# Second routed layer: the output projection made token-major in three passes, its additions on DVE

## The chip, the cores and the metric

The kernel runs on one core of a Trainium2 chip. The metric is the time of one execution in device microseconds (us), the median of several runs. The engines are PE (matrix products), DVE (vector), ACT (activations), POOL (general purpose) and SP, which issues the transfers.

## The reference, cut to what matters

The program is eight sublayers that add to x, 16 batch elements of 256 tokens of 128 numbers, 4096 tokens in all. The sixth one, the second routed layer, is concerned here. Each token has a routing weight rw for each of 16 experts, and every expert has 128 x 128 matrices for Q, K, V and the output:

```python
q = jnp.einsum('btc,ech,bte->bth', hidden_states, q_proj, rw)
k = jnp.einsum('btc,ech,bte->bth', hidden_states, k_proj, rw)
v = jnp.einsum('btc,ech,bte->bth', hidden_states, v_proj, rw)
scores = jnp.einsum('bqh,bkh->bqk', q, k) * scale      # causal, then a softmax over k
ao = jnp.einsum('bqk,bkh->bqh', attn, v)
out = jnp.einsum('bth,ehc,bte->btc', ao, o_proj, rw)   # added to x
```

## The kernel before

`layer2_ffn` works on groups of four tiles of 128 tokens, 512 tokens; there are eight groups (`ITERS`), j = 0 to 7. Each engine runs its own list of instructions in order, and they meet by counting signals. `run_mains` writes `main` out for the first two and the last two groups and loops over the four between.

In `main(j)` a loop over the experts e = 0 to 15 makes Q, K and V. PE spreads the routes of expert e over all partitions (`spread`, L1799, into one of the two banks psR), two experts ahead. DVE multiplies the transposed tokens by them (`scale_by`, L1980, into a ring of four buffers xs). ACT rounds the product to a high part xsh (L1727), and DVE writes the low part, xs - xsh (`low_part`, L1984), one expert later than the scaling. PE then adds nine products of 512 columns, three for each of Q, K and V: low weights by high tokens, high by low, high by high (L1865). Expert 0 has no parts: it takes three float32 products (L1860). Between the experts DVE makes the routes of the next group, in pieces at e = 6, 7, 8, 9, 11 and 13 (`front_gate` and what follows), and PE transposes for the next group at e = 2, 4 and 14.

After the loop comes the output projection of the group before, `mix_o(j)`. Again PE spreads the routes (a copy that POOL keeps, L1681), DVE scales the transposed attention result aoT by them, and PE makes one float32 product of 512 columns for each expert into psX (L1843). Put between these experts (`stages`) are the steps of this group's attention: scores, transposed V, the maxima and the normalised probabilities on DVE, their transposes, the product with V; and then, on DVE, the normalisation of group j + 2 (`front_ln`, `front_xn`, `front_norm`). ACT stores psX as oT, PE transposes it back to token-major at e = 10 of a later group (`out_T`, L1793), and DVE adds it to x (`add`, L2005). A last `mix_o(8)` stands behind the last group.

The weights are loaded during the attention sublayer that comes before (`narrow_attention`): SP starts the loads after its first `stack` of queries, and POOL makes the high and low parts of the Q, K and V weights (`Ahead.split`, L134 and L136) after its own last group.

Of the kernel before, what the change touches and what calls it, by code (L numbers as in the profile page):

```python
# [5 lines left out]
F32 = mybir.dt.float32  # L6
# [60 lines left out]
class Program:  # L67
# [19 lines left out]
    "dve_steps", "pool_steps", "act_steps", "ahead", "split", "up_scaled", "up_ready", "ctx_high", "ctx_split", "n_split", "q_split", "k_split", "khat_first", "x_split", "x_high", "x_loaded", "weights_qk", "inputs", "out_stored",  # L87
# [22 lines left out]
class Ahead:  # L110


    def __init__(self, tensors, loads, copies=(), splits=()):
        self.tensors, self.loads, self.copies, self.splits = tensors, loads, tuple(copies), tuple(splits)

    def __add__(self, other):
        return Ahead({**self.tensors, **other.tensors}, self.loads + other.loads, self.copies + other.copies,
                     self.splits + other.splits)
# [3 lines left out]


# [5 lines left out]
    def split(self, pr, pool):  # L129

        if self.splits:
            pool.wait_ge(pr.sig("ahead").sem, pr.sig("ahead").at(16 * len(self.loads)))
        for k, (raw, hi, lo) in enumerate(self.splits):
            pr.nc.gpsimd.tensor_copy(hi, raw).then_inc(pr.sig("split").sem, 1)  # L134
            pool.wait_ge(pr.sig("split").sem, pr.sig("split").at(k + 1))
            pr.nc.gpsimd.tensor_tensor(lo, raw, hi, ALU.subtract)  # L136

    @property
    def counts(self):
        return dict(ahead=16 * len(self.loads), split=len(self.splits))  # L140
# [447 lines left out]
def narrow_attention(pr, x_sb, common, dram, layer, wt, ahead):  # L588
# [7 lines left out]
    with ExitStack() as ctx:  # L596
# [28 lines left out]
        def _(sp):  # L625
# [18 lines left out]
            for j in range(ITERS):  # L644
                stack(j)
                if not j:
                    ahead.start(pr, sp)
                if masked and j + 1 < ITERS:
                    load_mask(j + 1)

        @block.gpsimd
        def _(pool):
# [14 lines left out]
            ahead.split(pr, pool)  # L667
# [903 lines left out]
def layer2_ffn_weights(nc, ctx, dram):  # L1571
    sb = buffers(nc, ctx, "f2w")
    E = L2_E
    t = {k: sb(k, [P, E, P]) for k in ("wq", "wk", "wv", "wo")}
    t.update(sim=sb("sim", [P, E]), ones=sb("ones", [P, P]), sg=sb("sg", [P, E]), desc=sb("desc", [P, E]),
             tri32=sb("tri32", [P, P]), tri=sb("tri", [P, P], BF16), self32=sb("self32", [P, E * P]),
             selb=sb("selb", [P, E * P], BF16))
    for k in ("wq", "wk", "wv"):
# [3 lines left out]
                     (t["tri32"][:], dram["tri"]), (t["self32"][:], dram["F2_sel"])] +  # L1582
                    [(t[k][:], dram["F2_" + k]) for k in ("wq", "wk", "wv", "wo")],
                 [(t["selb"][:], t["self32"][:]), (t["tri"][:], t["tri32"][:])],
                 [(t[k][:], t[k + "h"][:], t[k + "l"][:]) for k in ("wq", "wk", "wv")])


def layer2_ffn(pr, x_sb, common, wt):
# [8 lines left out]
    with ExitStack() as ctx:  # L1597
        def sb(name, shape, dt=F32):
# [3 lines left out]
        wq, wk, wv, wo, sim, ones, sg, tri, desc, selb = (wt[k] for k in ("wq", "wk", "wv", "wo", "sim", "ones", "sg", "tri",  # L1602
                                                                         "desc", "selb"))
# [9 lines left out]
        rwTo = sb("rwTo", [P, T4], BF16)  # L1613
# [7 lines left out]
        aoT, oT = sb("aoT", [P, 2, T4]), sb("oT", [P, T4])  # L1621
# [4 lines left out]
        psX = ctx.enter_context(nc.psum_tensor("psX_f2", [P, T4], F32))  # L1626
        psY = ctx.enter_context(nc.psum_tensor("psY_f2", [P, T4], F32))
        psA = psQKV + [psY]
# [7 lines left out]
        def qn(j, e):  # L1636
            return e if isinstance(j, int) and j == 0 else 2 * E * j - E + e

        def on(j, e):
            return 2 * E * j + e - (E if isinstance(j, int) and j == ITERS else 0)  # L1640


        def split_no(j, e):
            return (E - 1) * j + e - 1
# [21 lines left out]
        def _(pool):  # L1666
# [10 lines left out]
            def keep_routes(j, q):  # L1677

                pool.wait_ge(s("gate_bcast").sem, s("gate_bcast").at(2 * E * j + E))
                pool.wait_ge(s("gate_parts").sem, s("gate_parts").at(j + 1))  # L1680
                nc.gpsimd.tensor_tensor(rwTo[:].rearrange("e (c t) -> e c t", t=P), rwTb[:, q, :].rearrange("e (c t) -> e c t", t=P),  # L1681
                                        ones[:].unsqueeze(1).broadcast_to([P, TPI, P]), ALU.mult)\
                    .then_inc(s("routes_kept").sem, 1)

            def main(j, q):
                if has_second_next(j):
                    front(j + 2)
                keep_routes(j, q)
# [5 lines left out]
        def _(act):  # L1694
# [17 lines left out]
            def front_parts(j, q):  # L1712
                act.wait_ge(s("gate_T").sem, s("gate_T").at(j + 1))
                if not is_first(j, 2):
                    act.wait_ge(s("routes_kept").sem, s("routes_kept").at(j - 1))
                nc.scalar.activation(rwTb[:, q, :], psM[:], ACT.Copy).then_inc(s("gate_parts").sem, 1)

            def store_o(j):

                act.wait_ge(s("hidden").sem, s("hidden").at(on(j, E)))  # L1720
                act.wait_ge(s("ffn_outT_ready").sem, s("ffn_outT_ready").at(j - 1))
                nc.scalar.activation(oT[:], psX[:], ACT.Copy).then_inc(s("ffn_outT").sem, 1)

            def main(j, q):
                for e in range(1, E):
# [13 lines left out]
                for c in range(TPI):  # L1739
                    nk = P * (c % 2 + 1)  # L1740
                    act.wait_ge(s("maxed").sem, s("maxed").at(j * TPI + c + 1))
                    nc.scalar.activation(p[:, c, 0:nk], psA[c][:, 0:nk], ACT.Exp, bias=nmax[:, c:c + 1],
# [3 lines left out]
                for c in range(TPI):  # L1746
                    nk = P * (c % 2 + 1)
# [832 lines left out]
```

## Time and profile before

| | us |
|---|---|
| median of 3 runs | 2017.27 (2017.11 to 2026.06) |
| the profiled execution, its own time | 2015.44 |
| its span | 2013.3 |
| PE busy in the span | 1626.2 (81%) |
| DVE busy | 1284.4 (64%) |
| ACT busy | 926.6 (46%) |
| POOL busy | 210.0 (10%) |
| second routed layer, first instruction to last addition | about 1058 to 1613 |

Busy is the time in which an engine has an instruction under way. A matmul's record ends some time after the next one may start, so starts are compared rather than durations added. A float32 product of 512 columns is two records; a product of the rounded parts is one. The granted clock is the share of PE's full clock, 2.4 GHz; 0.50 is 1.2 GHz.

### The profile page before, as it was taken

To read this page: it belongs to the slowest core of one execution; us is meant where nothing else is said; L and a number is where in the kernel's file an instruction comes from. 1 tells how busy PE (TensorE), PEld (TensorE's weight loads), DVE (VectorE), ACT (ScalarE), POOL (GpSimd) and SP (SyncE) were. 2 spreads that over 40 slices of the span, in tenths; PEclk is the share of its full clock that TensorE was granted. 3 is DMA by queue.
4 is the path that set the end of the run, shared out by engine and by line. 5 is a ranking of instruction groups with operands and counts; after the bars stand their busy time and mean duration, and the time that the engine had idled before them with its cause. 6 is when DMAs were issued, how large, how long until landed. Compare 5 with 4: busy or idle time off the path is not lost. (4 is left out here: it accounts for less than half of the span.)

```text
span 2013.3 us, 27147 instructions
## 1 busy us (share of the span) xinstructions
PE 1626.2 (81%) x8633; PEld 1104.1 (55%) x8633; DVE 1284.4 (64%) x2870; ACT 926.6 (46%) x1759; POOL 210.0 (10%) x188
## 2 busy tenths in 40 slices
PE   6999938978869999978975899999999968848004
PEld 5777726855546666645653656656666445523004
DVE  4777771147657667646765566666665548776985
ACT  3555523356635565545551322222222146626862
POOL 2110020011200000011131000000000011010320
PEclk9999967959979999979996999999999969969557
DMA  4000000032100000023210000000000012100000
GB/s 149 1 1 0 0 1 0 0 112 47 39 1 0 1 0 0 1 91 104 60 26 0 1 1 0 1 1 0 0 1 0 0 50 50 43 0 0 0 0 42
DMA packets 23456, 41.71 MB, mean 21 GB/s; under 512 B 7720, under 2 KB 11184, under 8 KB 22320
## 3 DMA queue, kind: packets, MB, share of 16 engines
q1 hardware_dynamic: 23344, 40.32, 6.8%
q8 instruction: 58, 0.95, 0.2%
q14 instruction: 54, 0.44, 0.1%
HBM read 19.32 MB, written 2.10 MB: 11 GB/s over the span
## 5 line engine op out<-in xcount | busy, mean ns | idle before, releaser
L962 DVE TENSOR_REDUCE mP_a<-psY_a 128x8 f32<-128x512 f32 x192 | 128.2, 688 | 118.8 <-PE psY_a L800 117.9
L720 ACT ACTIVATE probs_a<-psX_a 128x512 f32<-128x512 f32 x192 | 109.1, 595 | 149.0 <-PE psX_a L827 148.3
L1727 ACT ACTIVATE xsh_f<-xs_f 128x512 fp32r<-128x512 f32 x120 | 75.8, 632 | 202.8 <-DVE xs_f L1980 202.6
L1980 DVE TENSOR_TENSOR xs_f<-xT_f,psR_f 128x512 f32<-128x512 f32 x128 | 86.9, 686 | 83.1 <-PE psR_f L1799 75.3
L1843 PE MATMUL psX_f<-xs_f,wo_f2w 128*128 128x512 f32 x256 | 128.6, 594 | 0.0
L2375 PE MATMUL ps_f<-wT_f,xq_f 128*128 128x128 f32 x192 | 24.5, 292 | 125.4 <-DVE xq_f L2396 125.4
L1980 DVE TENSOR_TENSOR xs_f<-aoT_f,psR_f 128x512 f32<-128x512 f32 x128 | 85.8, 685 | 61.6 <-PE psR_f L1799 61.4
L1507 DVE SCALAR_TENSOR_TENSOR g_f<-psU_f,cols_f1w,t_f 128x512 f32<-128x512 f32 (+1 forms) x104 | 77.9, 749 | 73.2 <-ACT t_f L1320 71.0
L800 PE MATMUL psY_a<-ks_a,xs_a 96*128 96x256 f32 x384 | 100.7, 367 | 28.0 <-DMA xs_a<-ql_a 16.3
L1402 PE MATMUL psO_f<-h_f,w_f1w 128*128 128x512 f32 (+1 forms) x208 | 107.6, 599 | 0.0
L1320 ACT ACTIVATE t_f<-psU_f,cols_f1w 128x512 f32<-128x512 f32 (+1 forms) x104 | 71.2, 684 | 76.0 <-PE psU_f L1386 76.0
L800 PEld LDWEIGHTS psY_a<-ks_a,xs_a 96*128 96x128 f32 x384 | 69.0, 215 | 59.6 <-issue 20.9
L827 PE MATMUL psX_a<-xs_a,ks_a 128*128 128x256 f32 x384 | 89.9, 336 | 10.2 <-ACT xs_a L712 10.2
L2375 PEld LDWEIGHTS ps_f<-wT_f,xq_f 128*128 128x128 f32 x192 | 23.8, 206 | 126.7 <-issue 126.7
L969 DVE RECIPROCAL heads_a<-psV_a 128x256 f32<-128x256 f32 x48 | 84.0, 1749 | 13.8 <-PE psV_a L840 13.8
L1984 DVE TENSOR_TENSOR xsl_f<-xs_f,xsh_f 128x512 fp32r<-128x512 f32 x120 | 82.5, 688 | 1.1
L827 PEld LDWEIGHTS psX_a<-xs_a,ks_a 128*128 128x128 f32 x384 | 66.8, 206 | 27.1 <-ACT xs_a L712 21.8
L1514 DVE TENSOR_TENSOR h_f<-act_h_f,psR_f 128x512 f32<-128x512 f32 (+1 forms) x104 | 70.5, 678 | 13.4 <-ACT act_h_f L1326 8.5
L179 POOL TENSOR_TENSOR rstd_f<-vareps_f,mhalf 128x4 f32<-128x4 f32 x16 | 16.2, 1010 | 580.1 <-DVE vareps_f L165 580.1
L376 ACT ACTIVATE vhat_a<-psF_a 64x256 f32<-64x256 f32 x122 | 46.1, 378 | 61.9 <-PE psF_a L434 61.1
L1865 PE MATMUL psQ_f<-xsh_f,wql_f2w 128*128 128x512 f32 x120 | 66.4, 554 | 5.0 <-DVE xsl_f L1984 4.9
L507 DVE TENSOR_REDUCE smax_a<-psS_a 128x16 f32<-128x1024 f32 x32 | 39.2, 1224 | 47.9 <-PE psS_a L441 47.9
(434 smaller groups left out, 4320.2 us busy)
## 6 DMA issues: line engine op xcount, KB each, us to landing
xs_a<-qh_a SPq DMA_DIRECT2D x192, 64.0 KB, 2.0
xs_a<-ql_a SPq DMA_DIRECT2D x96, 64.0 KB, 2.0
x_sb<-in_x SPq DMA_DIRECT2D x1, 2048.0 KB, 8.5
out<-x_sb SPq DMA_DIRECT2D x1, 2048.0 KB, 6.3
w_f1w<-in_F_w SPq DMA_DIRECT2D x2, 792.0 KB
ctxT<-in_ctxT SPq DMA_DIRECT2D x1, 1024.0 KB, 12.3
maskf_a<-in_mask SPq DMA_DIRECT2D x8, 128.0 KB, 2.3
maskf_a<-in_maskT SPq DMA_DIRECT2D x8, 128.0 KB, 2.5
```

The lines of the kernel that those rows point to most:

```text
L720: nc.scalar.activation(probs[:, b % 2, g, :, :], psX[g % 2][:].rearrange("p (e t) -> p e t", e=2), ACT.Exp, scale=float(dv) ** -0.5).then_ ...
L800: ins = nc.tensor.matmul(psY[h % 2][:, e * GK:(e + 1) * GK], xs[0:MAXROW, j % 2, g, t:t + P], ks[0:MAXROW, j % 2, p, g, :], start=not mask ...
L827: ins = nc.tensor.matmul(psX[g % 2][:, e * ST:(e + 1) * ST], ks[:, j % 2, p, g, e * P:(e + 1) * P], xs[:, j % 2, g, p * ST:(p + 1) * ST], ...
L962: nc.vector.tensor_reduce(mP[:, b % 2, h // 2, col:col + 8], psY[h % 2][:].rearrange("p (h k) -> p h k", h=8), axis=AX.X, op=ALU.max).then ...
L969: nc.vector.reciprocal(heads[:, b % 2, :], psV[:, ST:2 * ST]).then_inc(s("sums_inverted").sem, 1)
L1320: nc.scalar.activation(t3[r, g % 2, :], psU[g % 2][r, 1, :], ACT.Identity, bias=cols[r, CH + g % CH:CH + g % CH + 1])\
L1402: ins = nc.tensor.matmul(psO[:], w2[0:rows[k], k, :], h[0:rows[k], g % 2, :], start=False, stop=k == CH - 1)
L1507: nc.vector.scalar_tensor_tensor(g_[r, g % 2, :], psU[g % 2][r, 0, :], cols[r, k:k + 1], t3[r, g % 2, :], ALU.add, ALU.mult).then_inc(s("h ...
L1727: nc.scalar.activation(xsh[:, e % RING, :], xs[:, e % RING, :], ACT.Copy).then_inc(s("x_high").sem, 1)
L1843: nc.tensor.matmul(psX[:], wo[:, e, :], xs[:, e % RING, :], start=e == 0, stop=e == E - 1)\
L1980: nc.vector.tensor_tensor(xs[:, e % RING, :], src, psR[e % 2][:], ALU.mult).then_inc(s("scaled").sem, 1)
L1984: nc.vector.tensor_tensor(xsl[:, e % RING, :], xs[:, e % RING, :], xsh[:, e % RING, :], ALU.subtract)\
```

## The change

The output projection becomes token-major. A part k = 0 to 15 of group j is tile c = k // 4 and the four experts 4g to 4g + 3, g = k % 4. PE makes the part as three passes of 512 columns (high and low parts of the attention result by high and low parts of the output weights) into one of two banks psO. DVE then adds the four experts one after the other into x, each 128 columns, multiplied by the token's route as a column factor. Each of the four waits for the one before. So the scaling of the attention result, the second spreading of the routes, the store of psX, the transposes and the old addition go.

Parts 0 to 7 of group j - 1 are issued by PE in the expert loop of group j, after the passes of each odd expert, and DVE adds them at the even experts 2 to 14. Parts 8 to 15 stand after the loop, between the attention's steps. Expert 0 now has high and low parts like the others. The attention result is kept as a high part (ACT) and a low part (DVE). The attention's scores use three banks instead of four, in the order of tiles 0, 2, 1, 3. The selection matrix is one column an expert, read broadcast. In the attention sublayers POOL makes the first parts of the weights after its fifth group; two raw weight buffers are filled a second time (`refill`, on SP, at the seventh group), and four matrices get high and low parts instead of three.

```diff
     def refill(self, pr, sp):
+        for k, pair in enumerate(self.refills):
+            sp.wait_ge(pr.sig("split").sem, pr.sig("split").at(2 * k + 2))
+            load(sp, pr.sig("refilled"), [pair])
...
                 if not j:
                     ahead.start(pr, sp)
+                if j == ITERS - 2:
+                    ahead.refill(pr, sp)
...
                 layernorm_pool(pr, pool, j + 1, w)
                 add_bias(j)
-            ahead.split(pr, pool)
+                if j == ITERS // 2:
+                    ahead.split(pr, pool, 0)
+            ahead.split(pr, pool, 1)
...
-            def mix_o(j, attention):
-                pe.wait_ge(s("routes_kept").sem, s("routes_kept").at(j))
-                spread(on(j, 0), 0, rwTo[:])
-                spread(on(j, 1), 1, rwTo[:])
-                pe.wait_ge(s("ffn_outT").sem, s("ffn_outT").at(j - 1))
-                for e in range(E):
-                    if e + 2 < E:
-                        spread(on(j, e + 2), e + 2, rwTo[:])
-                    if e in attention:
-                        attention[e]()
-                    pe.wait_ge(s("scaled").sem, s("scaled").at(on(j, e + 1)))
-                    nc.tensor.matmul(psX[:], wo[:, e, :], xs[:, e % RING, :], start=e == 0, stop=e == E - 1)\
-                        .then_inc(s("hidden").sem, 1)
+            def mix_o(j, q, k):
+                c, g = k // 4, k % 4
+                pe.wait_ge(s("o_steps").sem, s("o_steps").at(4 * (OSTEPS * j + k - 1)))
+                for m, (left, right) in enumerate(((aol, woh), (aoh, wol), (aoh, woh))):
+                    ins = nc.tensor.matmul(psO[k % 2][:], left[:, q, c * P:(c + 1) * P], right[:, 4 * g:4 * g + 4, :], start=m == 0, stop=m == 2)
+                ins.then_inc(s("o_part").sem, 1)
...
-                    if e == 0:
-                        pe.wait_ge(s("scaled").sem, s("scaled").at(qn(j, 1)))
-                        for n, w32 in enumerate((wq, wk, wv)):
-                            ins = nc.tensor.matmul(psQKV[n][:], w32[:, e, :], xs[:, r, :], start=True, stop=False)
...
+                    pe.wait_ge(s("x_split").sem, s("x_split").at(qn(j, e + 1)))
+                    for n, (hi_w, lo_w) in enumerate(whl):
+                        for m, (wp, xp) in enumerate(((lo_w, xsh), (hi_w, xsl), (hi_w, xsh))):
+                            ins = nc.tensor.matmul(psQKV[n][:], wp[:, e, :], xp[:, r, :], start=e == 0 and m == 0, stop=e == E - 1 and m == 2)
                     ins.then_inc(s("hidden").sem, 1)
...
-                        out_T(j - 2)
+                    if not is_first(j, 1) and e % 2 == 1:
+                        mix_o(j - 1, 1 - q, e // 2)
...
+                some_o(IN_LOOP, 10)
+                scores(j)
+                v_to_tokens(j)
+                some_o(10, 13)
+                probs_T(j, 0)
+                probs_T(j, 1)
+                some_o(13, 15)
+                probs_T(j, 2)
+                probs_T(j, 3)
+                some_o(15, OSTEPS)
+                attend(j)
...
+            def attended_low(j, q):
+                dve.wait_ge(s("ao_high").sem, s("ao_high").at(j + 1))
+                nc.vector.tensor_tensor(aol[:, q, :], psM[:], aoh[:, q, :], ALU.subtract).then_inc(s("ao_ready").sem, 1)
+            def add_o(j, k):
+                c, g = k // 4, k % 4
+                xc = x_sb[:, bass.ds(j * TPI + c, 1), :].rearrange("p a d -> p (a d)")
+                dve.wait_ge(s("routes_kept").sem, s("routes_kept").at(j + 1))
+                dve.wait_ge(s("o_part").sem, s("o_part").at(OSTEPS * j + k + 1))
+                for m in range(4):
+                    e = 4 * g + m
+                    dve.wait_ge(s("o_steps").sem, s("o_steps").at(4 * (OSTEPS * j + k) + m))
+                    nc.vector.scalar_tensor_tensor(xc, psO[k % 2][:, m * P:(m + 1) * P], routes_o[:, c, e:e + 1], xc, ALU.mult, ALU.add)\
+                        .then_inc(s("o_steps").sem, 1)
             def main(j, q):
                 for e in range(E):
                     scale_by(qn(j, e), e, xT[:, q, :])
-                    if e > 1:
+                    if e > 0:
                         low_part(j, e - 1)
-                    if e == 12 and not is_first(j, 2):
-                        add(j - 2)
+                    if not is_first(j, 1) and e % 2 == 0 and e:
+                        add_o(j - 1, e // 2 - 1)
...
                 low_part(j, E - 1)
+                some_o(IN_LOOP - 1, 10)
+                maxima(j)
+                some_o(10, 11)
+                normalise(j, 0)
+                normalise(j, 1)
+                some_o(11, 12)
+                normalise(j, 2)
+                normalise(j, 3)
+                some_o(12, 14)
+                if has_second_next(j):
+                    front_ln(j + 2)
+                some_o(14, OSTEPS)
+                if has_second_next(j):
+                    front_xn(j + 2)
+                    front_norm(j + 2)
+                attended_low(j, q)
+                keep_routes(j, q)
```

`some_o(first, last)` issues the parts from first to last - 1, of the group before.

## Rows read from the trace of the kernel before

**Rows 1.** One iteration: span; busy of PE, PEld, DVE, ACT, POOL; clock; DMA.

```profile
1262.31:1327.16 64.85, 62.44 (x260) 40.65 (x259) 42.28 (x107) 18.58 (x45) 3.15 (x3) 1.00 0.00 1
```

**Rows 2.** Timeline of PE, two iterations: start us, us, line, operation.

```profile
1243.79 0.60 PE L1786 MATMUL psM_f<-ident,parts_f 128*128 128x128 f32 x4
...
1244.14 0.48 PE L1865 MATMUL psQ_f<-xsh_f,wql_f2w 128*128 128x512 f32 x1
...
1270.46 1.07 PE L1860 MATMUL psQ_f<-xs_f,wq_f2w 128*128 128x512 f32 x2
...
1301.91 0.58 PE L1865 MATMUL psQ_f<-xsh_f,wql_f2w 128*128 128x512 f32 x1
...
1304.25 0.58 PE L1865 MATMUL psQ_f<-xsh_f,wql_f2w 128*128 128x512 f32 x1
...
1308.99 0.48 PE L1865 MATMUL psQ_f<-xsh_f,wql_f2w 128*128 128x512 f32 x1
```

**Rows 3.** Timeline of DVE: two scalings, and two steps of the gate.

```profile
1071.17 0.23 DVE L1941 TENSOR_TENSOR lg_f<-psM_f,rn_f 128x64 f32<-128x64 f32 x1 [2.40 <-PE psM_f L1780]
...
1071.43 0.23 DVE L1942 TENSOR_TENSOR lg_f<-lg_f,sg_f2w 128x64 f32<-128x64 f32 x1
...
1300.50 0.68 DVE L1980 TENSOR_TENSOR xs_f<-xT_f,psR_f 128x512 f32<-128x512 f32 x1
...
1301.10 0.69 DVE L1984 TENSOR_TENSOR xsl_f<-xs_f,xsh_f 128x512 fp32r<-128x512 f32 x1
```

**Rows 4.** Timeline where PE waits for a low part.

```profile
1287.80 0.68 DVE L1984 TENSOR_TENSOR xsl_f<-xs_f,xsh_f 128x512 fp32r<-128x512 f32 x1
...
1288.54 0.51 PE L1865 MATMUL psQ_f<-xsh_f,wql_f2w 128*128 128x512 f32 x1
```

**Rows 5.** Timeline in the last output pass: one expert.

```profile
1595.15 0.69 DVE L1980 TENSOR_TENSOR xs_f<-aoT_f,psR_f 128x512 f32<-128x512 f32 x1 [0.39 <-PE psR_f L1799]
...
1595.80 0.38 PE L1799 MATMUL psR_f<-rwTo_f,selb_f2w 128*128 128x512 bf16 x1
...
1596.22 0.69 DVE L1980 TENSOR_TENSOR xs_f<-aoT_f,psR_f 128x512 f32<-128x512 f32 x1 [0.39 <-PE psR_f L1799]
```

**Rows 6.** Groups by line: count, then busy us, mean ns.

```profile
L1507 DVE SCALAR_TENSOR_TENSOR g_f<-psU_f,cols_f1w,t_f 128x512 f32<-128x512 f32 x96 | 72.0, 750 | 58.5 <-ACT t_f L1320 56.2 <-DVE oh_f L1039 0.7
...
L985 DVE TENSOR_TENSOR bo_a3w<-bo_a3w,psP_a 128x128 f32<-128x128 f32 x1 | 0.3, 281 | 0.0
```

**Rows 7.** Timeline of DVE: maxima, then normalisation of a later group.

```profile
1129.53 0.29 DVE L1991 TENSOR_REDUCE nmax_f<-psQ_f 128x1 f32<-128x128 f32 x1 [6.93 <-PE psQ_f L1814]
...
1133.00 0.86 DVE L156 BATCH_NORM_STATS2 stats_f<-x_sb 128x6 f32<-128x128 f32 x4
...
1135.80 1.11 DVE L171 TENSOR_SCALAR xn_f<-x_sb,mean_f,rstd_f 128x128 f32<-128x128 f32 x4 [1.12 <-POOL rstd_f L179]
...
1138.26 0.17 DVE L1935 TENSOR_SCALAR ssq_f<-ssq_f 128x4 f32<-128x4 f32 x1 [1.34 <-ACT sq_f L1701]
```

**Rows 8.** PE idle between groups of passes, and the granted clock by windows.

```profile
1139.08 0.61 PE L1799 MATMUL psR_f<-rwTb_f,selb_f2w 128*128 128x512 bf16 x1 [3.74 <-DVE xs_f L1980]
...
1649.06 0.47 PE L800 MATMUL psY_a<-ks_a,xs_a 96*128 96x256 f32 x2 [1.40 <-issue]
...
1136.00:1138.00 2.00, 0.00 (x0) 0.00 (x0) 0.92 (x4) 1.05 (x7) 0.00 (x0) 1.00 0.00 0
...
1138.00:1140.00 2.00, 0.92 (x2) 0.69 (x3) 1.64 (x4) 0.57 (x3) 1.49 (x2) 0.50 0.00 0
...
1144.00:1146.00 2.00, 2.00 (x7) 1.19 (x6) 0.86 (x2) 0.14 (x1) 0.00 (x0) 0.79 0.00 0
...
1650.00:1652.00 2.00, 1.66 (x12) 1.21 (x16) 0.95 (x2) 0.41 (x1) 0.00 (x0) 0.50 0.00 0
```

**Rows 9.** Second routed layer's attention: PE waiting for data, POOL making a low part.

```profile
916.18 0.61 PE L794 MATMUL psY_a<-maskb_a,identb 128*128 128x512 bf16 x1 [4.63 <-DMA xs_a<-ql_a]
...
1012.71 4.63 POOL L136 TENSOR_TENSOR wkl_f2w<-wk_f2w,wkh_f2w 128x2048 fp32r<-128x2048 f32 x1
```

More of the change, by code:

```diff
@@ L127, in convert, with first_splits, split @@
             pr.nc.scalar.activation(dst, src, ACT.Copy)
-    def split(self, pr, pool):
-        if self.splits:
+    @property
+    def first_splits(self):
+        return len(self.splits) - len(self.refills)
+    def split(self, pr, pool, part):
+        steps = range(self.first_splits) if part == 0 else range(self.first_splits, len(self.splits))
+        if steps:
             pool.wait_ge(pr.sig("ahead").sem, pr.sig("ahead").at(16 * len(self.loads)))
-        for k, (raw, hi, lo) in enumerate(self.splits):
+        for k in steps:
+            raw, hi, lo = self.splits[k]
+            if part:
+                pool.wait_ge(pr.sig("refilled").sem, pr.sig("refilled").at(16 * len(self.refills)))
             pr.nc.gpsimd.tensor_copy(hi, raw).then_inc(pr.sig("split").sem, 1)
-            pool.wait_ge(pr.sig("split").sem, pr.sig("split").at(k + 1))
-            pr.nc.gpsimd.tensor_tensor(lo, raw, hi, ALU.subtract)
+            pool.wait_ge(pr.sig("split").sem, pr.sig("split").at(2 * k + 1))
+            pr.nc.gpsimd.tensor_tensor(lo, raw, hi, ALU.subtract).then_inc(pr.sig("split").sem, 1)
     @property
     def counts(self):
-        return dict(ahead=16 * len(self.loads), split=len(self.splits))
+        return dict(ahead=16 * len(self.loads), split=2 * len(self.splits), refilled=16 * len(self.refills))
 def ln_buffers(sb):
@@ L1713, in front_parts @@
                 act.wait_ge(s("gate_T").sem, s("gate_T").at(j + 1))
-                if not is_first(j, 2):
-                    act.wait_ge(s("routes_kept").sem, s("routes_kept").at(j - 1))
                 nc.scalar.activation(rwTb[:, q, :], psM[:], ACT.Copy).then_inc(s("gate_parts").sem, 1)
[L1718 to L1722, printed above, removed]
             def main(j, q):
-                for e in range(1, E):
+                for e in range(E):
                     act.wait_ge(s("scaled").sem, s("scaled").at(qn(j, e + 1)))
@@ L1738, in main @@
                 nc.scalar.activation(qkvT[:, 2, :], psQKV[2][:], ACT.Copy).then_inc(s("qkv_ready").sem, 1)
[L1739 to L1742, printed above, removed]
+                for k, c in enumerate(ORDER):
+                    nk, (bank, off) = P * (c % 2 + 1), psA[c]
+                    act.wait_ge(s("maxed").sem, s("maxed").at(j * TPI + max(2, k + 1)))
+                    nc.scalar.activation(p[:, c, 0:nk], bank[:, off:off + nk], ACT.Exp, bias=nmax[:, c:c + 1],
                                          accum_out=rs[:, c:c + 1]).then_inc(s("probs").sem, 1)
@@ L1897, in _ @@
             pe.wait_ge(s("ao_ready").sem, s("ao_ready").at(ITERS))
[L1898 to L1901 removed]
+            for k in range(OSTEPS):
+                mix_o(ITERS - 1, 1, k)
         @block.vector
@@ L2033, in main, with some_o @@
                         elif e == 11:
-                            front_weights(j + 1, steps)
+                            front_weights(j + 1, steps, 1 - q)
                         elif e == 13:
-                            front_parts(steps)
+                            front_parts(steps, 1 - q)
                 low_part(j, E - 1)
-                stages = {1: lambda: maxima(j), 3: lambda: (normalise(j, 0), normalise(j, 1)),
-                          5: lambda: (normalise(j, 2), normalise(j, 3))}
-                if has_second_next(j):
-                    stages.update({10: lambda: front_ln(j + 2), 12: lambda: front_xn(j + 2), 14: lambda: front_norm(j + 2)})
-                if is_first(j, 1):
-                    for stage in stages.values():
-                        stage()
-                else:
-                    mix_o(j, 1 - q, stages)
+                def some_o(first, last):
+                    if not is_first(j, 1):
+                        for k in range(first, last):
+                            add_o(j - 1, k)
+                some_o(IN_LOOP - 1, 10)
[7 more added lines that the diff above has]
+                some_o(12, 14)
+                if has_second_next(j):
+                    front_ln(j + 2)
[5 more added lines that the diff above has]
+                keep_routes(j, q)
             front_ln(0)
```

186 lines of the change are left out of this document (74 added, 112 removed).

## The prediction

> **What bounds the kernel now.** I read the page, then the busy time of one whole iteration of the second routed layer, then the timelines of PE and of DVE in it. In the steady iteration PE is at work for 62.4 of 64.85 us at the full clock of 2.4 GHz, DVE for 42.3 [rows 1]. So the stage is bound by PE, and DVE has 22 us to spare. The starts of the first Q passes of two neighbouring experts lie 2.34 us apart: nine passes and one spreading of the routes, ten matmuls of 512 columns, 0.234 us each [rows 2]. I split the iteration at two points: from the first expert to the start of the last one is 38.5 us (1270.46 to 1308.99), from there to the next first expert 26.3 us (1244.14 to 1270.46) [rows 2]. I call these the loop and the outer part. In the outer part lie the attention and the old output projection, 1.07 us an expert [rows 5].
>
> **What PE gives back.** The old projection costs 16 x 1.07 = 17.2 us of PE. The new one costs 48 passes of 0.234 = 11.2. The first expert goes from three float32 matmuls of two hardware passes (2.6 us from 1270.46 to the next spreading) to nine passes, 2.1; the four transposes of the output, about 0.35 as those of the routes [rows 2], go. Together 7 us an iteration less. If PE stayed the bound, seven iterations with a projection inside them would give 49 us.
>
> **What the order of instructions does.** Here I chose to follow one pair of experts, and the forecast hangs on it. DVE takes its instructions in order. At an even expert e it scales e, writes the low part of e-1, and then waits for part k = e/2 - 1 of the projection. PE makes that part behind the nine passes of expert e-1, and those wait for the low part of e-1, which DVE has only just written. So DVE stands still for twelve passes, and the scaling of e+1 and the low part of e, which PE needs next, are queued behind the wait and behind four additions. Nothing covers them. The chain of one pair:
> - PE starts 0.06 us after a low part is written (1288.48 to 1288.54) [rows 4]. Twelve passes: eleven starts of 0.234 and a last record of 0.39, 2.96. DVE starts some 0.04 to 0.12 after it [rows 5]; I take 0.1.
> - Four dependent additions. No such operation is in the trace. A plain addition from PSUM at 128 columns took 0.281 us; a scalar_tensor_tensor with a column factor 0.750 at 512 columns [rows 6], where the plain operation took 0.69; that is 0.06 more, so 0.345. A dependent step starts 0.03 after the last one ended (0.23 long, 0.26 apart) [rows 3]. So 0.38 each, 1.52 for four. The bounds are 0.31 (the factor costs nothing) and 0.42.
> - Scaling and low part: 0.60 from start to start and 0.69 to the end, 1.29 [rows 3]. PE starts 0.06 later.
> - Nine passes, a spreading, and the next odd expert: 2.34. Its low part is ready by then (1.2 us of DVE).
>
> The sum is 0.06 + 2.96 + 0.1 + 1.52 + 1.29 + 0.06 + 2.34 = 8.3, against 2 x 2.34 = 4.7 now. Of the 3.7 more, 0.7 is the projection's three passes and 3.0 is PE standing still. Seven of the eight parts issued in the loop are waited for in it: 7 x 3.0 = 21 us. The gate's twelve steps at the even experts 6 and 8 are now uncovered: at 0.23 on average (some are independent), 2.7. Those at odd experts fit into the 2.34. The loop becomes 38.5 - 0.5 - 0.35 + 7 x 0.7 + 21 + 2.7 = 66.3.
>
> **The outer part.** From the start of the last expert's passes DVE can add after 3.1 us. Then it has nine parts at 1.52, 13.7; maxima and normalised probabilities, 3.5 with small waits (1129.53 to 1133.00), I take 3.0; the statistics of a later group, 1.7, and its normalisation, 1.0 [rows 7]; the wait for ACT's squares, 1.35, and one step, 0.1, which were covered and now have only the short low part behind them; the low part of the attention, 0.6; the kept routes, 0.2; two scalings and one low part, 1.9. Together 26.6, against 26.3. PE has parts 8 to 15 and the attention beneath it, so what it gave back there is gone. DVE is the clock of this part.
>
> One iteration: 66.3 + 26.6 = 92.9 against 64.85, 28.0 more, and 196 for seven. In the last two there is no group two ahead to normalise (about 4.2 us each: 1.7 + 1.0 + 1.45), and in the last no gate (2.7): -11. Before the first of the seven, +2: it starts with the attention's low part and waits for a low part, and saves 0.5. At the end, 16 parts at 1.52 + 1 = 25.3, against 27 for transposes and 16 experts: -2. That makes +185.
>
> **The attention before it.** The weights' low parts move: two of the three now follow POOL's work for the fifth group, and a fourth is added at its end (4.6 us for the subtraction, the copy is shorter) [rows 9]. They stand ahead of POOL's next reciprocal root and can make it some 6 us late; DVE uses that root a batch element, about half an iteration of this stage, after the statistics, so I count it as hidden, but only just. Without that cover DVE would be late by some 2 us, once. In the first routed layer the same move is of two shorter pairs. On SP two waits and two loads stand ahead of the last mask and the last stack, whose data are wanted an iteration later: hidden. The loads at the start fall from five of 1 MB to two, and PE waited 4.63 us for a stack behind them [rows 9]: I take -5, between 0 and -7. Now +180.
>
> **The clock.** PE fell to 1.2 GHz in an idle time of 3.74 us, before it ended: 1.00 in the window to 1138, 0.50 from there, and 1.00 again within the window from 1144 (0.79 in the mean) [rows 8]. PE worked some 5.7 us of that at half the clock, 2.8 lost. It also fell at 1650 after only 1.40 us idle, with more short idle time around it. The new idle times of 3.0 lie between these. The long one at each new iteration (DVE's last 8 us of the outer part) loses it surely: 7 x 2.3 = 16; I take 2.3 and not 2.8 since the fall can come later in the idle time and the rise sooner. The 49 in the loop: I take three in four at 2.25, 83; the bounds are 0 and 49 x 2.8 = 137. A rule bears on the choice. The Trainium skill (TensorE: Matmul & The Clock Gate, HAM oscillation — how this bites in real kernels) tells of a kernel whose repeated waits between bursts cost it the clock before every burst. By that rule all 49 would pay; its price is worked out among the rivals. The fall at 1138 agrees with it; no row here has repeated waits of 3 us.
>
> **Sum.** 180 + 16 + 83 = 279 us on the profiled execution's own 2015.4 (span 2013.3), 2294; the median of the runs is 2017.3, 2 above it: 2296.
>
> **The rivals.**
> - *The clock holds in the loop.* 2015.4 + 180 + 16, 2213 with the 2 us. For it: bursts of over 5 us between the idle times. Against it: the fall at 1650. Chance 0.18.
> - *It falls in every idle time of the loop.* 2213 + 49 x 2.25 = 2323, at 2.8 each 2350; with dearer additions (0.42 for 0.38, 64 x 8 of them, 20 us) and more queueing up to 2390. For it: the fall after 1.40 us. Against it: the fall at 1138 came some 2.7 us into its idle time, so 3.0 may just end in time. Chance 0.17. This is the case that the Trainium skill's section on the oscillation describes.
> - *The additions are hidden and the kernel is faster.* Were DVE to reach each wait only when the part is ready, the three passes would be all that the loop gains, and PE's 7 us an iteration would come back: 2017 - 49 - 5 = 1963; were DVE then the bound (64 additions 24.3, 32 scalings and low parts 19.2, the rest about 13: 57, near PE's 57.8), some 1985. The point that decides is the idle time of a pair: at 1.0 us (7 us an iteration) gain and loss are even, and I read 3.0. For it: DVE's 22 us to spare. Against it: the low part that DVE writes last is what the awaited passes need, so no lead of DVE can shorten the wait. Chance 0.06.
> - *Only the loop's chain is shorter than read,* by additions of 0.31 and less queueing in the outer part: 2150 to 2195. Chance 0.07.
>
> **How the numbers follow.** The forecast, 2296, has 0.50 and its own range is 2250 to 2320. The remaining 0.02 is the layer standing still much longer. Low end 2195: the clock holding (2213) with additions at 0.31 (64 x 8 x 0.07 = 36, half of it counted). High end 2390. Faster, within and slower share the cases: faster only where the additions are hidden, 0.06; within 0.5%, about 10 us and what a measurement can tell, 0.01; slower 0.93.
>
> **What would show it.** Right: between the passes of an odd and of the next even expert PE idle for about 3 us, released by DVE's low part; DVE idle some 3 us ahead of the first of each four additions, released by PE; 0.345 us an addition; 92 us and more an iteration; the clock at 0.6 to 0.9 in the stage; PE no more waiting 4.6 us for a stack. Wrong: iterations under 65 us, or DVE's wait ahead of the additions under 1 us.

## The result, and the profile after

The changed kernel takes 2306.5 us (median of four runs, 2299.5 to 2308.2) against 2017.7 for the kernel before on the same chip: ratio 1.141, 95% interval 1.138 to 1.145, 289 us slower. The forecast was 2296, its own range 2250 to 2320. The profiled execution of the changed kernel has a span of 2306.1 us.

The second routed layer's stage, from POOL's clearing of `parts` to the end of the last additions, grows from 554.5 us (1058.32 to 1612.78) to 832.4 (1073.60 to 1905.98), by 278. Some 11 us come in the attention layers, 4 before the first of them. One iteration of the changed kernel by windows (columns as in [rows 1]; it starts where DVE begins the attention's low part):

```profile
1361.40:1466.66 105.26, 73.40 (x254) 53.87 (x258) 53.69 (x157) 18.27 (x44) 2.01 (x2) 0.81 0.00 1
```

Against [rows 1] the iteration is 105.3 us long instead of 64.9, PE idles 32 us of it, the clock is 0.81, and DVE's work has grown by 11.4 us without filling its time. The seven iterations take 95 to 110 us. Split as the prediction splits them, by the starts of the experts' first passes (the loop from the first expert to the last, the outer part from there to the next first expert), six of the seven loops take 76 to 81 us where they took 38 to 40 before, and the outer parts 26.5 to 26.7 where they took 26.2 to 26.3 (one takes 29.8 where it took 28.0, the last is shorter). So the added time lies in the loop. Two groups of the whole kernel:

```profile
L1997 DVE SCALAR_TENSOR_TENSOR x_sb<-psO_f,routes_o_f,x_sb 128x128 f32<-128x128 f32 (+1 forms) x512 | 179.4, 350 | 342.2 <-PE psO_f L1825 207.8 <-issue 115.9 <-DVE x_sb L1997 0.6
...
L1842 PE MATMUL psQ_f<-xsh_f,wql_f2w 128*128 128x512 f32 x128 | 83.1, 649 | 160.9 <-DVE xsl_f L1962 160.9
```

An addition takes 0.350 us (0.345 was taken from [rows 6]), and 342 us of idle time stand ahead of the additions, 208 of them put down to PE. PE idles 161 us ahead of the first pass of an expert, all of it released by DVE's low part. Each engine waits for the other. The timeline of one pair, DVE's rows and then PE's:

```profile
1426.10 1.51 DVE L1997 SCALAR_TENSOR_TENSOR x_sb<-psO_f,routes_o_f,x_sb 128x128 f32 x4 [4.94 <-PE psO_f L1825]
1427.53 0.68 DVE L1958 TENSOR_TENSOR xs_f<-xT_f,psR_f 128x512 f32<-128x512 f32 x1
1428.12 0.69 DVE L1962 TENSOR_TENSOR xsl_f<-xs_f,xsh_f 128x512 fp32r<-128x512 f32 x1
...
1436.03 1.51 DVE L1997 SCALAR_TENSOR_TENSOR x_sb<-psO_f,routes_o_f,x_sb 128x128 f32 x4 [4.97 <-PE psO_f L1825]
```

```profile
1425.49 0.40 PE L1825 MATMUL psO_f<-woh_f2w,aoh_f 128*128 128x512 f32 x1
1425.73 0.39 PE L1785 MATMUL psR_f<-rwTb_f,selb_f2w 128*128 128x512 bf16 x1
1428.86 0.50 PE L1842 MATMUL psQ_f<-xsh_f,wql_f2w 128*128 128x512 f32 x1 [2.74 <-DVE xsl_f L1962]
...
1431.02 0.63 PE L1842 MATMUL psQ_f<-xsl_f,wvh_f2w 128*128 128x512 f32 x1
1431.45 0.63 PE L1842 MATMUL psQ_f<-xsh_f,wvh_f2w 128*128 128x512 f32 x1
```

The last projection pass ends at 1425.9; four additions, a scaling and a low part follow on DVE, and 0.05 us after the low part PE goes on, where [rows 4] have 0.06. The passes at 1431 are 0.43 us apart instead of 0.23. The granted clock, by windows:

```profile
1428.00:1430.00 2.00, 1.14 (x5) 0.96 (x6) 1.90 (x9) 0.63 (x1) 0.00 (x0) 1.00 0.03 8
1430.00:1432.00 2.00, 2.00 (x7) 1.20 (x6) 1.06 (x2) 0.63 (x1) 0.00 (x0) 0.52 0.00 0
1432.00:1434.00 2.00, 2.00 (x6) 1.61 (x7) 0.00 (x0) 0.00 (x0) 0.00 (x0) 0.63 0.00 0
```

PE stood idle up to 1428.86, worked again at 2.4 GHz, fell to 1.2 GHz at about 1430 while busy, and rose some 3 us later. The fall comes behind the idle time, not in it as in [rows 8]. The trace has 49 such waits of over 2 us for a low part. Behind 33 of them (2.6 to 3.0 us long) the clock falls up to 1.55 us after PE has resumed, at 12 longer ones (3.3 to 5.2 us) it falls before, and at 4 (2.6 to 2.9 us) it holds. One of the four, a wait of 2.62 us up to 1220.10:

```profile
1220.00:1224.00 4.00, 3.90 (x16) 3.04 (x18) 2.20 (x9) 0.73 (x2) 0.00 (x0) 1.00 0.00 0
```

In the attention sublayer ahead of this layer, POOL's rows, then DVE's, then PE's:

```profile
960.20 1.89 POOL L147 CAST wkh_f2w<-raw_f2w 128x2048 fp32r<-128x2048 f32 x1
962.17 4.49 POOL L149 TENSOR_TENSOR wkl_f2w<-raw_f2w,wkh_f2w 128x2048 fp32r<-128x2048 f32 x1
967.03 1.14 POOL L192 TENSOR_TENSOR rstd_a<-vareps_a,mhalf 128x4 f32<-128x4 f32 x1 [0.36 <-DVE vareps_a L178]
```

```profile
960.83 1.29 DVE L173 TENSOR_TENSOR mv_a<-stats_a 128x4 f32<-128x4 f32 x1
...
962.29 4.40 DVE L176 TENSOR_SCALAR mean_a<-mv_a 128x4 f32<-128x4 f32 x1
...
966.87 0.43 DVE L952 TENSOR_SCALAR maskb_a<-maskf_a 128x512 bf16<-128x512 int32 x1
...
978.00 1.10 DVE L184 TENSOR_SCALAR xn_a<-x_sb,mean_a,rstd_a 128x128 f32<-128x128 f32 x4
...
987.82 0.17 DVE L176 TENSOR_SCALAR mean_a<-mv_a 128x4 f32<-128x4 f32 x1
```

```profile
967.55 0.58 PE L811 MATMUL psY_a<-maskb_a,identb 128*128 128x512 bf16 x1 [6.64 <-DVE maskb_a L952]
```

An operation of 128x4 that takes 0.17 us a group later takes 4.40 here and ends at 966.69, within 0.03 us of the end of POOL's subtraction (966.66); the one before it ends at 962.12, with POOL's copy (962.09). POOL's root starts at 967.03. It could not have come before 966.66, when the subtraction ends, so it is late by POOL's queue as well; but its result is first read by DVE at 978.00, some 10 us after it is there, so this lateness is covered. What is not covered is DVE's own queue: behind the held operation stands the mask, written at 966.87, and PE waits 6.64 us for it. PE's wait of 4.63 us for a stack [rows 9] is 1.77 us now; the two waits of this kind before it are unchanged (4.00 and 2.74 before, 3.99 and 2.73 now).

### The profile page after: what moved, and what is told of

The parts are those of the page before. It is cut to its first block and busy times, and to the rows that moved or that the text cites. A ratio compares the mean times of both kernels' runs of the same rounds, so it can differ in the third digit from the quotient of the medians.

```text
span 2306.1 us, 27697 instructions
## 1 busy us (share of the span) xinstructions
PE 1691.0 (73%) x8575; PEld 1187.2 (51%) x8625; DVE 1384.3 (60%) x3270; ACT 922.3 (40%) x1759; POOL 207.4 (9%) x182
## 5 line engine op out<-in xcount | busy, mean ns | idle before, releaser
L1997 DVE SCALAR_TENSOR_TENSOR x_sb<-psO_f,routes_o_f,x_sb 128x128 f32<-128x128 f32 (+1 forms) x512 | 179.4, 350 | 342.2 <-PE psO_f L1825 207.8
L1721 ACT ACTIVATE xsh_f<-xs_f 128x512 fp32r<-128x512 f32 x128 | 80.5, 631 | 468.3 <-DVE xs_f L1958 468.3
L1842 PE MATMUL psQ_f<-xsh_f,wql_f2w 128*128 128x512 f32 x128 | 83.1, 649 | 160.9 <-DVE xsl_f L1962 160.9
L1842 PEld LDWEIGHTS psQ_f<-xsh_f,wql_f2w 128*128 128x128 f32 x128 | 30.4, 238 | 177.8 <-DVE xsl_f L1962 172.0
L1825 PE MATMUL psO_f<-woh_f2w,aol_f 128*128 128x512 f32 x128 | 57.8, 452 | 44.5 <-DVE x_sb L1997 42.7
L1962 DVE TENSOR_TENSOR xsl_f<-xs_f,xsh_f 128x512 fp32r<-128x512 f32 x128 | 87.7, 685 | 1.5
L1785 PE MATMUL psR_f<-rwTb_f,selb_f2w 128*128 128x512 bf16 x98 | 44.3, 452 | 36.6 <-DVE xs_f L1958 35.2
```

The source lines that it names most:

```text
L1721: nc.scalar.activation(xsh[:, e % RING, :], xs[:, e % RING, :], ACT.Copy).then_inc(s("x_high").sem, 1)
L1842: ins = nc.tensor.matmul(psQKV[n][:], wp[:, e, :], xp[:, r, :], start=e == 0 and m == 0, stop=e == E - 1 and m == 2)
L1962: nc.vector.tensor_tensor(xsl[:, e % RING, :], xs[:, e % RING, :], xsh[:, e % RING, :], ALU.subtract)\
L1997: nc.vector.scalar_tensor_tensor(xc, psO[k % 2][:, m * P:(m + 1) * P], routes_o[:, c, e:e + 1], xc, ALU.mult, ALU.add)\
```

## The experiments

Ratios are to the kernel before on the same chip. "In the loop" is the loop over the 16 experts.

**Additions one expert later.** Only the place of DVE's additions moves.

```
-  if not is_first(j, 1) and e % 2 == 0 and e:
+  if not is_first(j, 1) and e % 2 == 1 and e > 1:
       add_o(j - 1, e // 2 - 1)
```

> Inside the loop over experts DVE adds part k behind the scaling of odd expert 2k+3 instead of even expert 2k+2; nothing else moves. Lockstep theory (PE waits for a low part that stands behind additions that wait for PE's own passes): both waits go, the loop is then PE's own 39 us plus some 2 to 3 of gate steps, the iteration 67 to 69 us instead of 95 to 110, PE's clock holds in the loop, and the kernel takes 2030 to 2060 us. Rival A (the additions' own work on DVE is what costs, wherever it stands): the iteration stays at 95 to 105 us and the kernel over 2250. Rival B (the chain goes, but the clock falls at the waits that are left in the outer part): 2100 to 2150.

Measured: 2115.1 us, ratio 1.047 (1.045 to 1.050), 191 us less than the changed kernel with the same instructions. Rival A falls. The seven loops together are 189 us shorter, the outer parts as long as they were (26.5 to 26.7 us), so the whole gain lies where the lockstep was. But 2030 to 2060 was missed. The expectation's 39 us for PE's own loop left out the parts' passes (42.5 with them), and waits are left: six of the loops take 49 to 52 us, with 1.4 to 1.9 us of PE idle ahead of experts 7, 9, 11 and 13. PE's idle time ahead of an expert is 47 us in all (161 in the changed kernel), and the long ones between iterations stay. The time lies in the range of rival B, but the clock does not explain the miss: PE's work at half clock in the loops is 3 to 7 us an iteration, and 3 to 6 in the run with additions three experts later, which is 61 us faster. The rows:

```profile
1388.81 0.61 PE L1785 MATMUL psR_f<-rwTb_f,selb_f2w 128*128 128x512 bf16 x1 [6.98 <-DVE xs_f L1958]
...
1429.70 0.51 PE L1842 MATMUL psQ_f<-xsh_f,wql_f2w 128*128 128x512 f32 x1 [1.53 <-DVE xsl_f L1962]
```

**Work that is thrown away, in PE's idle time.** The added matmuls write into the bank whose additions are long done, so they start as soon as PE has no other work; their results are overwritten.

```
   if e == 0:
       pe.wait_ge(s("pT_ready").sem, ...)
+  if not is_first(j, 1) and e % 2 == 0 and e:
+      pe.wait_ge(s("o_steps").sem, s("o_steps").at(4 * (OSTEPS * (j - 1) + e // 2 - 1)))
+      for _ in range(10):
+          nc.tensor.matmul(psO[e // 2 % 2][:], selb[:, e:e + 1].broadcast_to([P, P]), rwTb[:, q, :], start=True, stop=True)
   r = e % RING
```

> The changed kernel with work added that is thrown away: ten 128x512 matmuls (10 x 0.213 = 2.1 us at full clock) into the free bank of the projection at each even expert from 2 on, ahead of the passes that wait for the low part some 2.7 to 3.0 us. Clock theory (PE's idle stretch between the experts is what makes the clock fall): the clock holds in the loop, the three-pass groups go back from a mean of 490 ns to near 215 a pass, the kernel takes 2215 to 2250 although PE does 14 per cent more instructions. Rival A (the clock falls for another reason): the added work at half clock is 4.3 us, more than the idle time, and the kernel takes 2350 to 2390. Rival B (the clock costs little, the chain is what takes the time): 2295 to 2315.

Measured: 2225.3 us, ratio 1.102 (1.099 to 1.105): 81 us less than the changed kernel, with 490 matmuls more. The clock theory stands: PE is idle 53 us ahead of the experts instead of 161, and 77 of the 81 us are gained in the seven loops. A pair in it:

```profile
1481.18 2.32 PE L1841 MATMUL psO_f<-rwTb_f,selb_f2w 128*128 128x512 bf16 x10
1484.16 0.49 PE L1846 MATMUL psQ_f<-xsh_f,wql_f2w 128*128 128x512 f32 x1 [0.65 <-DVE xsl_f L1966]
...
1492.45 0.50 PE L1846 MATMUL psQ_f<-xsh_f,wql_f2w 128*128 128x512 f32 x1 [0.52 <-DVE xsl_f L1966]
```

From 1484.16 to 1492.45 is 8.29 us: the forecast's chain of a pair, 8.3, at the full clock. It is the shortest; the later three pairs of an iteration take 8.3 to 8.5, the first three, with gate steps on DVE in two of them, 8.8, 9.9 and 10.9. Six of the loops take 66 to 68 us, the outer parts 26.5 to 26.7 (one 29.2). Over 300 us in the stage the clock is 0.94, against 0.81 in the changed kernel.

**All weight splits at the end of attention.** SP's refills go behind its loop as well.

```
       for j in range(ITERS):
           layernorm_pool(pr, pool, j + 1, w)
           add_bias(j)
-          if j == ITERS // 2:
-              ahead.split(pr, pool, 0)
+      ahead.split(pr, pool, 0)
       ahead.split(pr, pool, 1)
```

> All weight splits of POOL behind its loop over groups, in both attention layers, as in the kernel before; SP's refills behind its loop too. Theory (POOL's long copies and subtractions in the middle of attention hold back DVE's small operations: 4.40 us for one that takes 0.17, 3.47 in layer 1): 10 to 14 us less than the changed kernel, 2292 to 2297, with the attention layers' end back within 4 us of before. Rival (the later end of attention in the changed kernel came from its loads or from one run to the next): no change, 2303 to 2309.

Measured: 2289.3 us, ratio 1.134 (1.132 to 1.137). Less than the changed kernel by 0.7% in the ratio, some 14 us, with some 9 either way by the two intervals. The stage that follows begins at 1055.5 instead of 1073.6; 3.6 us of that lie before the first attention layer, where the two programs do the same. One trace against another can differ by such amounts. But in the four traces with the splits in the middle the stage begins at 1070.0 to 1073.6, in the eight with the splits at the end (the kernel before among them) at 1055.2 to 1064.0. SP's refills were moved along with the splits here; the next run moves the splits alone. A layer norm's step and a later multiplication on DVE in this kernel, then a subtraction of POOL at the end:

```profile
969.75 0.17 DVE L176 TENSOR_SCALAR mean_a<-mv_a 128x4 f32<-128x4 f32 x1
...
1006.03 0.42 DVE L986 TENSOR_TENSOR heads_a<-psV_a,heads_a 128x256 f32<-128x256 f32 x1
```

```profile
1002.19 4.54 POOL L149 TENSOR_TENSOR wql_f2w<-raw_f2w,wqh_f2w 128x2048 fp32r<-128x2048 f32 x1
```

At the end DVE has no 128x4 steps of a later group left beside POOL; the multiplication with one input in PSUM starts and ends inside POOL's subtraction in 0.42 us, as elsewhere. PE waits 1.29 us for the mask, where it was 6.64 in the changed kernel:

```profile
970.78 0.38 PE L809 MATMUL psY_a<-maskb_a,identb 128*128 128x512 bf16 x1 [1.29 <-DVE maskb_a L950]
```

**The same move in the kernel before.** One line: the call behind group 5 instead of behind the loop.

> The kernel before, with the one edit that POOL's weight splits stand behind group 5 of attention instead of behind the last group. Theory (POOL's splits hold DVE's small operations back there): slower by 8 to 14 us, 2025 to 2031, ratio 1.004 to 1.007, with DVE operations of 128x4 of 3 to 4.6 us beside the splits. Rival (hidden, as the prediction had it): no change, or up to 2 us more in all.

Measured: 2028.7 us, ratio 1.0052 (1.0035 to 1.0068), 10.5 us slower by the ratio. The mechanism is there without the rest of the change:

```profile
961.17 1.90 POOL L134 CAST wvh_f2w<-wv_f2w 128x2048 fp32r<-128x2048 f32 x1
```

```profile
956.86 4.40 DVE L163 TENSOR_SCALAR mean_a<-mv_a 128x4 f32<-128x4 f32 x1
...
961.35 1.74 DVE L165 SCALAR_TENSOR_TENSOR vareps_a<-mv_a 128x4 f32<-128x4 f32 x1
```

The last row, two SBUF inputs, ends at 963.09, with POOL's copy at 963.07.

**Additions three experts later, splits at the end.** The splits and SP's refills stand as two runs above; the additions:

```
-  if not is_first(j, 1) and e % 2 == 0 and e:
-      add_o(j - 1, e // 2 - 1)
+  if not is_first(j, 1) and e % 2 == 0 and e > 2:
+      add_o(j - 1, e // 2 - 2)
```

> Two edits: DVE adds part k at even expert 2k+4, three experts behind its passes (the run with one expert later still left PE 1 us or so idle per pair, since its passes were waited for while the low part of the next odd expert stood behind the additions), and all weight splits at attention's end. Lockstep theory: the loop over experts is PE's own passes, 46 to 48 us instead of 53 with one expert later and some 66 to 70 in the changed kernel, the iteration 69 to 72 us; with the 14 to 17 us of the splits the kernel takes 2035 to 2065 us. Rival (DVE's total work bounds the iteration once its additions are there): no faster than the run with one expert later but for the splits, 2095 to 2105.

Measured: 2054.2 us, ratio 1.017 (1.014 to 1.021). PE's idle time ahead of an expert is 14 us in all, the iteration 71 us with DVE at work for 54 of them, and the lockstep is gone. The loop takes 43 to 45 us instead of the 49 to 52 with one expert later; by the seven loops' sum that is 45 of the 61 us gained, and the splits give the rest. What is left over the kernel before: the loop is 5.4 us longer in the mean of the seven, since seven parts' passes in it are 4.9 us of PE's work, and the outer part, 26.5 us, is as long as before although PE has less to do there (7.28 us of PE idle at 1351.15).

**Three more parts in the loop.** The passes stand behind experts 1, 3, 5, 7, 9 and 10 to 15, the additions at experts 4, 6, 8 and 10 to 15.

> As the run that adds at even expert 2k+4 with the splits at the end, and three more of the 16 parts are multiplied inside the loop (behind experts 1, 3, 5, 7, 9 and each from 10 to 15), the added parts two or three experts behind, so that five instead of eight are left beside the softmax. Theory (the stretch outside the loop is bound by DVE, which has 14 us of additions in 25 us there, while PE bounds the loop and DVE idles some 2 us a pair in it): the loop grows by 2 us, the stretch outside falls by 4 to 5, the iteration is 2 to 3 us shorter, and the kernel takes 2015 to 2050. Rival (DVE's gate steps and additions together become the bound of the loop): 0 to 20 us slower than that run.

Measured: 2065.1 us, ratio 1.022 (1.019 to 1.026): the rival. The outer part falls by 2.4 us, as DVE has fewer additions there, but the loop grows by 3 to 4. The iteration is 72.0 us with PE idle 0.9 to 1.2 at the experts of the gate's steps; what leaves DVE's outer part comes back in the loop, and DVE has as much to do.

**The next iteration's first expert early.** To the run with additions three experts later. On DVE `front_norm`, the end of a later group's normalisation, also moves behind the attention's low part and the kept routes:

```
   v_to_tokens(j)
+  if not is_last(j):
+      spread(qn(j + 1, 0), 0, rwTb[:, 1 - q, :])
+      spread(qn(j + 1, 1), 1, rwTb[:, 1 - q, :])
...
   some_o(14, OSTEPS)
+  if not is_last(j):
+      scale_by(qn(j + 1, 0), 0, xT[:, 1 - q, :])
+      scale_by(qn(j + 1, 1), 1, xT[:, 1 - q, :])
+      low_part(j + 1, 0)
```

> As the run that adds at even expert 2k+4 with the splits at the end; and the first expert's work of the next iteration (spreads 0 and 1 on PE, scalings 0 and 1 and low part 0 on DVE, high part 0 on ACT) stands ahead of the attention output's low part, where PE sat idle 7.28 us between two iterations. Theory (that wait is a chain through DVE's queue, not work that is missing): 5 to 6 us less per iteration, 71.4 to 66, the kernel 2005 to 2025. Rival (DVE, busy 53.7 of 71.4 us, only finds the same work at another place): 2045 to 2055.

Measured: 2035.3 us, ratio 1.008 (1.006 to 1.011), 19 us less: under 3 us an iteration, between theory and rival; which of the two moves gave it was not tried. The steady iteration is 67.6 us with DVE busy 53.9.

**The route's factor on ACT, the sum on DVE.** Eleven parts stand in the loop, the splits at the end, the first expert early, as in the runs above. `scale_o` on ACT takes the place of `add_o`, `sum_o` on DVE adds up each four parts:

```
+  for m in range(4):
+      e = 4 * g + m
+      ins = nc.scalar.activation(ys[:, c % 2, e, :], psO[k % 2][:, m * P:(m + 1) * P], ACT.Copy, scale=routes_o[:, c, e:e + 1])
...
+  nc.vector.tensor_reduce(osum[:], ys[:, c % 2, :, :].rearrange("p e d -> p d e"), axis=AX.X, op=ALU.add)
...
+  nc.vector.tensor_tensor(xc, osum[:], xc, ALU.add)
```

> A version that the runs point to: passes and spreads as in the two runs before it (eleven parts in the loop, splits at the end, first expert early), but the 64 route-times-output steps of an iteration go to ACT (busy 18 of 71 us), which reads the bank and writes the scaled tiles to SBUF, and DVE sums 16 of them at once into x (4 reductions of 2048 and 4 additions of 128 instead of 64 operations of 0.35 us). Theory (with the lockstep gone DVE's work is what bounds): DVE 54 to about 40 us per iteration, PE the bound again at 58 to 61 us per iteration, the end 10 us shorter, the kernel 1960 to 1990, faster than both. Rival (ACT's copies for the softmax and the high parts queue up behind its new work): 2005 to 2050.

Measured: 2035.1 us, ratio 1.008 (1.005 to 1.011), a miss. The time lies in the range of the rival, but what the trace shows is something else. The reductions take 3.73 us in the mean where 2.2 was reckoned, and three of the four stand outside the loop, the third and fourth ahead of low parts that PE waits for; DVE's row and what it holds on PE:

```profile
1275.59 3.58 DVE L2026 TENSOR_REDUCE osum_f<-ys_f 128x128 f32<-128x2048 f32 x1
...
1280.86 0.79 PE L1873 MATMUL psQ_f<-xsh_f,wql_f2w 128*128 128x512 f32 x1 [5.43 <-DVE xsl_f L1995]
```

**Those two sums later.** `sum_o(j - 2, 2)` and `sum_o(j - 2, 3)` at experts 2 and 4 of the next iteration.

> As the run with ACT's scaling, but the sums of the third and fourth 16 tiles stand behind low parts 1 and 3 of the next iteration instead of ahead of its first low parts: there the reductions, 3.6 to 3.8 us each where 2.2 was reckoned, held PE idle for 5.43 us and lengthened the stretch outside the loop. Theory: 5 to 7 us less per iteration (68 to 62), the kernel 1985 to 2005, faster than both. Rival (the sums only move the wait to expert 4): 2025 to 2040.

Measured: 2009.2 us, ratio 0.995 (0.993 to 0.997), 26 us less for the same work; 2005 was narrowly missed.

**The experts innermost.** ACT writes `ys[:, c % 2, :, e]`, so that the 16 experts' values lie side by side, and DVE reads `ys[:, c % 2, :, :]`.

> As the run before it, but the scaled tiles lie with the 16 experts innermost, so that each reduction reads neighbouring elements and ACT writes with a stride of 64 bytes. If the stride over experts is what makes a reduction of 2048 take 3.6 to 3.8 us, it falls to about 2.2 and the kernel to 1975 to 2000; if it is not, or if ACT's 128x128 steps grow from 0.27 us by a like amount, no gain over the run before it.

Measured: 1985.3 us, ratio 0.983 (0.981 to 0.985): 1.7% faster than the kernel before and 14% than the changed one.

```profile
L1725 ACT ACTIVATE ys_f<-psO_f,routes_o_f 128x128 f32<-128x128 f32 x512 | 159.0, 501 | 67.7 <-PE psO_f L1855 59.8 <-issue 4.3 <-DVE x_sb L2029 3.5
L2026 DVE TENSOR_REDUCE osum_f<-ys_f 128x128 f32<-128x2048 f32 x32 | 72.9, 2280 | 9.4 <-ACT ys_f L1725 9.3
```

```profile
1257.67:1317.39 59.72, 55.78 (x260) 42.34 (x259) 42.43 (x102) 34.93 (x109) 2.02 (x2) 1.00 0.00 1
```

A reduction takes 2.28 us, ACT's total grows from 146 to 159. The iteration is 59.7 us, 5.1 less than [rows 1]; PE is at work for 55.8 of them at the full clock, 6.7 us less than before: of the 7 us that the new projection gives back, 5.1 arrive in the iteration.

## Why the prediction was right, step by step

- **The chain of a pair, 8.3 us.** Shown. With PE kept busy it measures 8.3 to 8.5 in the later pairs, and moving the additions alone takes 191 us away. The additions were 1.51 for the 1.52 taken. The first three pairs are longer, by some 4.5 us together, where 2.7 were counted for the gate's steps.
- **DVE's idle time "some 3 us" ahead of the additions.** Too short: 5.6 in the mean of the 49 in the changed kernel (3.3 to 8.3), 4.3 with PE kept busy. DVE has mostly written the odd expert's low part while PE is still in the even expert's passes, so it waits for their rest as well as for the twelve that follow; only where gate steps keep DVE at work until then is it as short as 3.2 to 3.5. The sum of the chain had this (it counts 2.34 for the even expert's passes), the sentence on the wait did not.
- **An iteration of 92.9 us.** With the clock nearly held (0.94), in the run with thrown-away work, five of the seven take 93 to 96 us and the last two, where work falls away, 90 and 82 (from one keeping of the routes to the next), 644 in all for the 639 predicted without the clock (7 x 92.9 less 11). Its two parts fit as well: the loop 66 to 68 for 66.3, the outer part 26.5 to 26.7 for 26.6. At the changed kernel's clock the iterations take up to 110.
- **The clock, 83 us in the loop.** That the clock is what costs is shown, and so is the size: filling the idle times gave 81 back. An estimate from the passes agrees: all but the first pass of an expert average 0.48 us in the changed kernel, between 0.395 at 2.4 GHz and 0.63 at 1.2, so about 37% of these 1024 ran slow; taken for all 1152 high and low passes, at 0.19 more each, that is some 80 us. The factors behind the 83 are another matter. "Three in four at 2.25" stands for 37 waits that pay; counted in the trace it is 45 of the 49, so each cost about 81 / 45 = 1.8 us. One factor was too low and the other too high, and that they make the right product is luck. The reason given for the waits that do not pay, that 3.0 us may just end in time, fails: behind waits of 2.6 to 3.0 us the clock mostly falls after PE has resumed. The rival in which the clock holds would have been 2213; the experiment that nearly makes it hold (0.94) gives 2225. The rule that was weighed, of the Trainium skill (TensorE: Matmul & The Clock Gate, HAM oscillation — how this bites in real kernels), by which all 49 would pay, is nearly borne out; the rival built on it, 2323, had its price per wait too high. The 16 us for the long wait of each new iteration have no experiment of their own.
- **The move of the weights' splits, "hidden, but only just".** This is the step that failed. Instead of nothing, and -5 for the loads, the attention layers take 11 us more, and the two experiments put 14 and 10.5 us on the splits. The forecast looked at POOL's queue, where the root would be late, and there its cover held: the root's result lay some 10 us unread. What it left out are DVE's own 128x4 steps, which stand still until POOL's copy or subtraction ends, with the mask that PE waits for behind them. Of the -5 for the loads some 3 us are seen: the one wait went from 4.63 to 1.77 us. The Trainium skill (SBUF — State Buffer, Who interferes with whom) has this: DVE and GpSimd share one pair of ports, which an instruction holds to its end, and DVE contends for it in its two-port modes, and with two SBUF inputs against a GpSimd instruction that reads SBUF. The rows agree: the held operations end with POOL's instruction to 0.03 us, and those with an input in PSUM are not held (0.42 us inside POOL's subtraction). That the ports are the cause is the page's account; the runs show only who is held, and until when.
- **Additions hidden and kernel faster, 0.06.** Not for this order, and the deciding point was named rightly as the idle time of a pair. "No lead of DVE can shorten the wait" was true only with the additions at that place; put behind one or three experts more they wait for a part that is long done. But the rival's 1985 for a kernel in which DVE's additions are the bound was not reached: with the additions on DVE the best is 2035, still above the kernel before. The last version comes to 1985 by another way, with 11 us of DVE's work gone and PE the bound, and the equal number is chance.
- **The sum.** 185 + 99 = 284 was predicted for the stage and 278 measured; -5 for attention against +11. The errors cancel in part: 2296 against 2306.5. The remaining 4 us, ahead of the first attention layer, belong to no step here.

## What to carry to other kernels

When a result is consumed on an in-order engine whose next instructions feed the producer, count the chain round both queues, not the busy time: DVE had 22 us an iteration to spare, and the order of its queue still cost 191 us. The cure is one line, consuming the result an expert or three later, and the waits that then remain show where work has to move. It removed the loss and made no gain: the kernel got faster than before only after work had left DVE. Long elementwise work on POOL belongs where DVE has no small SBUF operations, whatever POOL's own queue allows.

## What the runs showed that was not expected

- Holding DVE can have a tail. In the kernel before with the splits in the middle, the two groups after the held ones come 20.49 us apart instead of 18.94, with the granted clock at 0.93 where it was 1.00. In the changed kernel, with a like hold, they come 18.94 apart again. What makes the difference was not tried.
- A fall of the clock can come over 1 us after PE has resumed work (idle to 1428.86, fall at about 1430, up again within 1432 to 1434).
- DVE's reduction over 16 tiles costs 3.73 us for 2048 elements when they lie 512 bytes apart and 2.28 when they are neighbours; ACT's writes 64 bytes apart cost 0.50 against 0.39 us an operation.
- PE matmuls that compute nothing bought 81 us.
